# Layer 3 of the top network in four column groups of TensorE, with the weight column padded to 32

## The reference

```python
e = jnp.stack([tbl_0[ids[:, 0]], ..., tbl_25[ids[:, 25]]], axis=1)      # 2048 x 26 x 128
all_vecs = jnp.concatenate([dense_proj[:, None, :], e], axis=1)         # 2048 x 27 x 128
interactions = jnp.einsum('bnd,bmd->bnm', all_vecs, all_vecs)
z = concatenate([dense_proj, upper triangle of interactions], axis=1)   # 128 + 351
h = concatenate([z, dense_proj], axis=1)                                # 607
h = maximum(h @ W_top1 + b_top1, 0)                                     # 512
h = maximum(h @ W_top2 + b_top2, 0)                                     # 256
y = h @ W_top3                                                          # 1
```

## Time and profile before

| what | value |
|---|---|
| median of three executions | 378.46 us (377.51 to 379.61) |
| the profiled execution's own time | 377.73 us |
| its span in the trace | 375.8 us |
| PE (matmuls) | 340.7 us busy, 91% of the span |
| PEld (weight loads) | 311.5 us, 83% |
| VectorE | 241.1 us, 64% |
| GpSimd | 244.4 us, 65% |
| ScalarE | 140.8 us, 37% |
| mean granted TensorE clock | 0.991 |

### The profile page before, as it was taken

How to read it: one execution, slowest core, us unless ns; L and a number is a source line. 1 busy time by engine, 2 the same in 40 slices (tenths; PEclk the granted TensorE clock), 3 DMA queues, 4 the chain that set the end, 5 groups by cost and what they waited for, 6 DMA issues and landing times.

```text
span 375.8 us, 14270 instructions
## 1 busy us (share of the span) xinstructions
PE 340.7 (91%) x6096; PEld 311.5 (83%) x6096; DVE 241.1 (64%) x702; ACT 140.8 (37%) x232; POOL 244.4 (65%) x260
## 2 busy tenths in 40 slices
PE   0575789969999999999999999999999999999797
PEld 0574779969998898998989998998989998997675
DVE  4989997976564885648565885659564985602210
ACT  2265232424422452435413442435422551436032
POOL 5357777777777777777777777777767777770000
PEclk9999998998999999999999999999999999999999
DMA  6999934232235221532135121531234112310000
GB/s 191 283 239 240 287 89 127 63 119 54 55 92 184 55 53 51 151 119 56 49 82 189 50 57 49 153 115 49 54 97 168 49 49 56 77 49 9 19 2 0
DMA packets 16566, 36.90 MB, mean 98 GB/s; under 512 B 5461, under 2 KB 8541, under 8 KB 16543
## 3 DMA queue, kind: packets, MB, share of 16 engines
q1 hardware_dynamic: 8335, 19.77, 17.8%
q0 software_dynamic: 8192, 16.79, 17.0%
q10 hardware_dynamic: 16, 0.01, 0.0%
HBM read 36.54 MB, written 0.01 MB: 97 GB/s over the span
## 4 chain that ended last, share of the span: by engine, by line
PE 84%; DVE 7%; DMA 4%; issue 3%; SPq 2%; ACT 1%; POOL 1%; DVEq 0%
PE hid L390 13%; PE gram L416 13%; PE look_ps L344 8%; PE look_odd L344 7%; PE look_odd L346 7%; PE look_ps L346 7%; PE vec_act L317 7%; PE hid L397 7%; DVE onehot L560 4%; PE hid L344 4%; PE hid L346 4%; DMA raw<-tbl 3%; DVE look_lo L568 2%; PE small L359 1%; PE small L406 1%
## 5 line engine op out<-in xcount | busy, mean ns | idle before, releaser
L300 POOL DMA_INDIRECT vecs<-tbl,ids_sb x256 | 244.2, 954 | 93.0 <-issue 75.6
L560 DVE TENSOR_SCALAR onehot<-step_ids,row_no 125x256 fp32r<-125x256 int32 x640 | 198.3, 379 | 81.2 <-PE look_ps L346 35.5
L535 ACT COPY vecs_T<-vec_act 128x512 f32<-128x512 f32 x64 | 46.2, 731 | 110.6 <-PE vec_act L317 110.6
L344 PE MATMUL look_odd<-onehot,look_hi 125*128 125x256 f32 x256 | 67.4, 300 | 5.6 <-DVE look_lo L568 5.6
L344 PE MATMUL look_ps<-onehot,look_hi 125*128 125x256 f32 x256 | 68.1, 301 | 1.6 <-DVE look_lo L568 1.6
L346 PE MATMUL look_ps<-onehot,look_lo 125*128 125x256 f32 x256 | 64.0, 285 | 0.0
L346 PE MATMUL look_odd<-onehot,look_lo 125*128 125x256 f32 x256 | 62.9, 282 | 0.0
L416 PE MATMUL gram<-vecs_T 128*27 128x26 f32 x4096 | 53.0, 192 | 6.5 <-issue 3.9
L416 PEld LDWEIGHTS gram<-vecs_T 128*27 128x27 f32 x4096 | 44.4, 104 | 15.8 <-issue 9.6
L344 PEld LDWEIGHTS look_odd<-onehot,look_hi 125*128 125x128 f32 x256 | 48.7, 190 | 6.7 <-DVE look_lo L568 6.4
L344 PEld LDWEIGHTS look_ps<-onehot,look_hi 125*128 125x128 f32 x256 | 49.1, 192 | 2.3 <-DVE look_lo L568 1.8
(11 more groups left out here) (70 smaller groups left out, 282.4 us busy)
## 6 DMA issues: line engine op xcount, KB each, us to landing
step_ids<-look_ids SPq DMA_DIRECT2D x15, 640.0 KB
raw<-tbl SPq DMA_DIRECT2D x10, 448.0 KB
vecs<-tbl,ids_sb POOLq DMA_INDIRECT x256
dense_new<-dense SPq DMA_DIRECT2D x8, 128.0 KB
dense_T<-dense SPq DMA_DIRECT2D x8, 128.0 KB, 2.7
raw<-tbl SPq DMA_DIRECT2D x10, 52.0 KB
step_ids<-look_ids SPq DMA_DIRECT2D x1, 512.0 KB
w_sb<-w SPq DMA_DIRECT2D x1, 512.0 KB
```

The costliest lines, as they stand in the source:

```text
L300: nc.gpsimd.indirect_dma_start(out=vecs[j][:, k, :], out_offset=None, in_=tables[k], in_offset=bass.IndirectOffsetOnAxis(ap=ids_sb[:, t, k ...
L344: nc.tensor.matmul(bank, look_hi[:, f, ch, :], onehot[:, i % SLOTS, c, :], start=ch == 0, stop=False)
L535: return engine_copy(vecs_T[j][:, :, lo:lo + GROUP], bank[:, :, :].rearrange("d v b -> d b v"))
L560: last = nc.vector.tensor_scalar(onehot[:, i % SLOTS, c, :], step_ids[a][0:LOOK_K, f - a * LOOKUPS // 2, :], row_no[0:LOOK_K, ch:ch + 1], ...
```

## The change

Layer 3's 256 samples are cut into four quarters of 64. Quarter `g` is multiplied in column group `g` of the array and lands at PSUM partition 32 `g`. For that the weight column is laid out as 32 columns, the first of which is the weight and the others zeros, so that each quarter fills 32 partitions of PSUM; the results stand in partitions 0, 32, 64 and 96. In place of two matmuls of 256 columns there are eight of 64 (`c` outside, `g` inside). ScalarE copies 128 partitions by 64 columns in place of 1 by 256, and the output DMA takes four rows of 64 numbers in place of one row of 256; the output tensor has the shape 32 x 64 in place of 1 x 2048, with the numbers in the same order. The load of the weight moves 32 KB in place of 1 KB.

```diff
+Y_PARTS = P // QUAD
-        y_row = raw[1][0:1, 0:PAIR]
+        y_rows = raw[1][:, 0:PAIR // Y_PARTS]
-        w3_sb = sb("w3_sb", [P, H2 // P])
+        w3_sb = sb("w3_sb", [P, H2 // P, QUAD])
-        y_ps = small[0:1, 0:PAIR]
+        y_ps = small[:, 0:PAIR // Y_PARTS]
-        y_ends = [hid1[0:1, 0, :], look_odd[0:1, 0:PAIR]]
+        y_ends = [hid1[:, 0, 0:PAIR // Y_PARTS], look_odd[:, 0:PAIR // Y_PARTS]]
-                load_weight(w3_sb[:, :], w3)
+                load_weight(w3_sb[:, :, :].rearrange("p c n -> p (c n)"), w3)
+                def layer3_parts(bank):
+
+                    for c in range(H2 // P):
+                        for g in range(Y_PARTS):
+                            last = nc.tensor.matmul(bank[g * QUAD:(g + 1) * QUAD, :], w3_sb[:, c, :],
+                                                    h2_T[:, c, g * PAIR // Y_PARTS:(g + 1) * PAIR // Y_PARTS],
+                                                    start=c == 0, stop=c == H2 // P - 1)
+                    return last
+
                 def layer3(m, bank=y_ps):
                     pe.wait_ge(h2_copied, m + 2)
                     if bank is y_ps:
                         pe.wait_ge(pairs_copied, 2 * m + 3)
-                    for c in range(H2 // P):
-                        last = nc.tensor.matmul(bank, w3_sb[:, c:c + 1], h2_T[:, c, :],
-                                                start=c == 0, stop=c == H2 // P - 1)
-                    last.then_inc(y_ready, 1)
+                    layer3_parts(bank).then_inc(y_ready, 1)
                 pe.wait_ge(h2_copied, pairs + 2)
-                for c in range(H2 // P):
-                    end = nc.tensor.matmul(y_ends[1], w3_sb[:, c:c + 1], h2_T[:, c, :], start=c == 0, stop=c == H2 // P - 1)
-                end.then_inc(y_ready, 1)
+                layer3_parts(y_ends[1]).then_inc(y_ready, 1)
-                    nc.scalar.copy(y_row, bank).then_inc(y_copied, 1)
+                    nc.scalar.copy(y_rows, bank).then_inc(y_copied, 1)
                     act.wait_ge(y_copied, m + 2)
-                    act.dma_start(out[:, bass.ds(m * PAIR, PAIR)], y_row).then_inc(y_out, 16)
+                    act.dma_start(out[bass.ds(m * Y_PARTS, Y_PARTS), :], y_rows[0:P:QUAD, :]).then_inc(y_out, 16)
```

More of the change, by code:

```diff
@@ L799 @@
         "b2": np.ascontiguousarray(np.asarray(inputs["b_top2"]).reshape(H2 // P, P).T),
-        "w3": np.ascontiguousarray(np.asarray(inputs["W_top3"]).reshape(H2 // P, P).T),
+        "w3": np.ascontiguousarray(np.pad(np.asarray(inputs["W_top3"]).reshape(H2 // P, P).T[:, :, None],
+                                          ((0, 0), (0, 0), (0, QUAD - 1))).reshape(P, -1)),
         "fold_mask": np.ascontiguousarray(np.broadcast_to(
@@ L811 @@
           for name, a in arrays.items()}
-    out = nc.dram_tensor("y", (1, dense.shape[1]), F32, kind="ExternalOutput").ap()
+    out = nc.dram_tensor("y", (dense.shape[1] * Y_PARTS // (2 * P), 2 * P // Y_PARTS), F32, kind="ExternalOutput").ap()
     build(nc, ap["dense"], ap["ids"], ap["look_ids"], [ap[f"tbl_{f}"] for f in large],
```

## The result

The changed kernel has a median of 376.47 us over 14 executions (375.4 to 378.34), the kernel before 379.34 over 14 beside it (377.2 to 382.01). The ratio is 0.9931, 95% interval [0.9905, 0.9956]: 2.6 us less (1.7 to 3.6). The forecast was 4.1 us less. The direction is right, and the size was forecast more than half as large again as it is. The profiled execution took 375.73 us, with a span of 373.8, which is 2.0 us less than before. Of these 2.0 us, 0.94 lie ahead of the first layer 3 (it starts at 127.03 us in place of 127.97), where the change alters nothing that PE computes.

A forecast was written before the change was run, and what follows sets the result against it. PE's streaming was taken to bound the kernel; 2.95 (loop) + 0.59 + 0.59 (last two layers 3) + 0.16 (copy) - 0.2 (stalls) = 4.1 us less, 378.46 to 374.4 us; range 372.6 to 376.7, the forecast's own 373.3 to 375.5.

The forecast's parts named there:

- The price of layer 3: Layer 3 on PE: 0.36 to 0.37 us in place of 0.96, a gain of 0.59 us for each that counts.
- the 17.3 ns of the earlier trace: Gram matrices before the change: a pair of 26-column passes took 17.3 ns, read as column groups running side by side.
- in order: Layer 3: every pass holds back those behind it, so 0.64 us a layer, 2.3 us gained, 376.1 us; chance 0.15.
- no overlap: Layer 3: column groups don't overlap, 0.15 us more for each of seven layers, 379.4 us; chance 0.07.
- Which layers count: PE's loop: five of six layers 3 shorten the time, as no engine is late behind them; 5 x 0.59 = 2.95 us.
- The term of 2.95 us: Gain forecast for five layers 3 in the loop, 0.59 us each.
- The sixth counts for nothing: Loop's last layer 3: PE waits for VectorE's fold behind it, 0.4 us growing to 1.0, so no gain.
- Pair 6: Layer 3 behind the loop, among full-width matmuls, with no engine named as late: gain 0.59 us.
- Pair 7: Last layer 3, alone on the path: gain 0.59 us, ScalarE's copy 0.16 more, output DMA unchanged (-0.1 to +0.3).
- Stalls of the instruction supply: PE around layer 3: 24 added instructions may arrive too slowly; 0.2 us lost in all, bounds 0 to 1.9.
- the stop at 353 us: PE's 2.24 us standstill in a gram block behind the loop; a changed length was to show the prediction wrong.
- starved: A 0.27 us instruction gap falls into or behind each layer 3: gain 2.4 us, 376.1 us; chance 0.12.

The follow-up runs named there:

- the second trace of the changed kernel: The changed kernel run again, unaltered, beside the others on one chip; ratio 0.9931 [0.9891, 0.9971] to the kernel before.
- with the fold early: Last look-up unit moved behind layer 3, VectorE transposing one unit earlier, against the kernel before: four groups 375.72 us (0.9896), old layer 3 380.22 us (1.0012).

## Why the prediction was right or wrong

- **The price of layer 3**: right to 0.01 us. The last of 16 matmuls starts at 0.211 us (forecast 0.214), the way back to full width is kept, 0.36 us in all. The groups run side by side, as the 17.3 ns of the earlier trace rows said; the rivals "in order" (0.64 us) and "no overlap" are out. Where nothing slows the layer, the 16 starts come in four rounds of four, 6 to 12 ns apart within a round and 31 to 55 ns from the last of one round to the first of the next. The Trainium skill's page "TensorE: Matmul & The Clock Gate" (section "Wait — 56ns, not 53.3ns?") gives about 25 ns as the least distance between starts. The trace disagrees for these matmuls in four column groups: 16 starts lie within 211 ns. (In the forecast's estimate by that page, 0.40 us in place of 0.27 would leave a gain of 0.46 us and not 0.44; the sum did not use it.)
- **Which layers count**: this step failed. "Five of the six in the loop: behind each comes a look-up unit whose one-hot matrices were made during the tile before". That was true, and I asked of every engine whether it would be late, but not of PE's own sequencer. The rows before show a matmul 0.10 us behind the last pass, and I read that as the way back alone. Under the 0.95 us lay some 0.75 us of sequencer work for the turn of the loop, and after it the look-up's first matmul; layer 3 could only shrink to 0.86 to 0.95. The term of 2.95 us was 0.26, and 0.7 in the second trace of the changed kernel (209.5 us for the five turns). The distance from layer 3 to the next matmul, summed over the five turns, fell by only 0.25 and 0.31 us; the rest of the 0.7 is in the gram blocks.
- **The sixth counts for nothing**: right. The wait for the fold went from 0.4 to 0.9 us.
- **Pair 6**: 0.59 us, right. **Pair 7**: from layer 3's start to the copy 0.50 us where 0.47 was forecast and 1.06 stood before; the copy 0.21 us (forecast 0.20). But the DMA took 0.47 us more, outside the bounds of -0.1 to +0.3, so the end gained 0.24 us of 0.75.
- **Stalls of the instruction supply**: 0.2 us was set down for layer 3 itself. No gap of 0.27 us stands inside it in any turn; in the slower turns the last start moves out to 0.24 us. That the short stops come from the supply of instructions was a reading that no run shows; in the turns from 130 us on no code is loaded on q8 while they occur. But the stops matter elsewhere: in the gram blocks they give back a third to a half of what PE saves in a turn (33.7 to 35.1 us of gram matrices, with the fold early), and the shorter wait for code behind the loop was worth 0.5 to 1 us to this change, which no step of the forecast had. "The prediction is wrong if the stop at 353 us changes its length" stood in the text; it did.

The sum as it came, by the traces: turns 0.3 to 0.7, the stretch with the stop 0.5, pair 6 0.59, the end 0.24: 1.6 to 2.0 us, against 2.6 measured (1.7 to 3.6). The stretch is the mean from the loop's last layer 3 to pair 6's, 24.4 us in the five traces with the old body and no other change there, 23.9 in the two of the changed kernel. It varies by 1 us among executions of one kernel, and so does what lies ahead of the first layer 3, and so what is left isn't assigned. That the measured median of 376.47 us lies inside the stated range of 372.6 to 376.7 is luck in part: the range reached so far for the rivals "in order" and "starved", both of which would have given 376.1 us, and the traces bear out neither. The forecast's own range, 373.3 to 375.5, leaves it out, and what took the 2.7 us from the turns was in no rival.

## What to carry to other kernels

What streams last in a loop's body covers the turn of the loop on that engine's sequencer: the branch, the register set-up and the waits at the head, which end 0.75 us behind layer 3's start here. Before shortening it, ask what else lies under it; afterwards end the body with something long, or close the loop at a place that streams. A wait named in the profile can be the sequencer's own lateness, and unrolling, or moving the branch, tells. A loop's body on PE has a length beyond which each jump back costs several microseconds (between about 1550 instructions, which were held, and twice as many, which weren't). This output DMA cost more in four pieces of 256 bytes than in one of 1 KB. And before the difference of two traces is laid on a change, see how much of it stands where nothing was changed: 0.94 of 2.0 us here.

## What was not expected of the hardware

- Column groups of a small fp32 matmul overlap nearly in full: 16 MATMULs of 64 columns, two passes each, start within 211 ns, where four of 256 columns need 645 ns for the same work.
- The turn of a loop costs PE 0.62 to 0.67 us when the body ends with 9 ns matmuls, nothing visible when it ends with 0.86 us of streaming. With a body of about twice 1550 instructions the branch back alone takes 3.9 and 4.2 us, while code is loaded again.
- 24 useless PE instructions a turn made a kernel 1.6 us faster (ratio 0.9958 [0.9931, 0.9985]), while they moved a stop of 2.0 to 3.1 us behind the loop to a place where it lasted 1.7 us (1.1 to 1.7 in the changed kernels). The stop is a wait for a 16 KB load of code and ends 1.2 to 1.5 us after it.
- An output of 1 KB in four pieces of 256 bytes ends 0.5 us later than in one piece, from one partition as from four.
